# V's product in the recurrence as four 32x32 tiles on the diagonal instead of one 128x128 matmul

## The reference, cut to what matters

```
Wx = x @ W.T, normalised over all B*T rows, scaled by gamma, shifted by beta
Vt = V.T                                 # 32 x 32
def step(yt, wx_t):
    yt = sigmoid(wx_t + yt @ Vt)
    return (yt, yt)
_, ys = scan(step, zeros(B, H), Wx in order of t)
```

## Time and profile before

| | us |
|---|---|
| median of 3 runs | 905.27 (901.69 to 906.05) |
| the profiled execution, its own time | 901.04 |
| its span, first to last instruction | 899.3 |
| mean granted TensorE clock over the span | 0.956 of full speed |
| TensorE matmul busy (PE) | 708.9 (79%) |
| VectorE busy (DVE) | 721.3 (80%) |
| GpSimd busy (POOL) | 516.2 (57%) |
| ScalarE busy (ACT) | 369.3 (41%) |

### The profile page before, as it was taken

How to read it: one execution, slowest core, us unless ns; L and a number is a source line. 1 busy time by engine, 2 the same in 40 slices (tenths; PEclk the granted TensorE clock), 3 DMA queues, 4 the chain that set the end, 5 groups by cost and what they waited for, 6 DMA issues and landing times. The chain is left out here.

```text
span 899.3 us, 19137 instructions
## 1 busy us (share of the span) xinstructions
PE 708.9 (79%) x7722; PEld 442.3 (49%) x7722; DVE 721.3 (80%) x938; ACT 369.3 (41%) x585; POOL 516.2 (57%) x407
## 2 busy tenths in 40 slices
PE   7987886699877387788878878887887787787696
PEld 3554553356554154544544544454454454446363
DVE  3998887763320489999999989999999999974998
ACT  2220002156536755545555555555455554321000
POOL 5000000000010489999999999999999999970043
PEclk9999998889989799999999999999999999998799
DMA  4000000000004256666666665666667666600001
GB/s 162 5 4 4 5 4 2 3 1 1 1 1 126 74 171 210 197 187 190 212 194 188 197 203 177 189 209 196 189 189 213 187 198 205 195 30 1 0 12 41
DMA packets 55866, 102.81 MB, mean 114 GB/s; under 512 B 11169, under 2 KB 13345, under 8 KB 55777
## 3 DMA queue, kind: packets, MB, share of 16 engines
q1 hardware_dynamic: 55552, 100.73, 36.6%
q0 software_dynamic: 224, 0.85, 0.2%
HBM read 98.00 MB, written 3.54 MB: 113 GB/s over the span
## 5 line engine op out<-in xcount | busy, mean ns | idle before, releaser
L546 POOL TENSOR_TENSOR ring<-ring,big 128x576 f32<-128x576 f32 x206 | 285.1, 1406 | 13.7 <-DVE ring L936 11.8
L184 PE MATMUL banks<-ring,main_params 128*128 128x288 f32 x824 | 244.2, 426 | 4.6 <-POOL ring L546 2.8
L936 DVE TENSOR_TENSOR_SCAN ring<-big,banks 128x576 f32<-128x576 f32 x154 | 202.6, 1340 | 2.3
L184 PEld LDWEIGHTS banks<-ring,main_params 128*128 128x128 f32 x824 | 146.4, 192 | 60.0 <-POOL ring L546 15.7
L924 DVE TENSOR_TENSOR banks<-banks,big 128x576 f32<-128x576 f32 x192 | 143.0, 745 | 24.0 <-PE banks L1218 21.4
L718 ACT ACTIVATE big<-big,small 128x576 f32<-128x576 f32 x192 | 142.2, 764 | 27.3 <-DVE ring L936 21.5
L523 POOL COPY big<-normed 128x288 f32<-128x288 f32 x8 | 3.0, 429 | 244.2 <-DVE normed L422 244.2
L1217 PE MATMUL banks<-big,selectors 96*128 96x512 bf16 x192 | 74.5, 390 | 80.0 <-DVE ring L936 37.4
L356 PE MATMUL banks<-big 32*32 32x288 f32 x3712 | 96.9, 429 | 21.3 <-issue 17.2
L790 DVE SCALAR_TENSOR_TENSOR big<-big 128x288 f32<-128x288 f32 x216 | 93.6, 512 | 0.0
L718 ACT ACTIVATE banks<-big,small 128x576 f32<-128x576 f32 x64 | 47.4, 741 | 108.2 <-DVE ring L936 86.9
(11 more groups left out here) (166 smaller groups left out, 962.5 us busy)
## 6 DMA issues: line engine op xcount, KB each, us to landing
big<-bc_rows SPq DMA_DIRECT2D x640, 144.0 KB, 3.2
bc_rows<-big SPq DMA_DIRECT2D x16, 144.0 KB, 2.4
residual<-x_in SPq DMA_DIRECT2D x2, 576.0 KB, 5.8
out<-big SPq DMA_DIRECT2D x2, 512.0 KB, 3.0
main_params<-main_in SPq DMA_DIRECT2D x1, 895.0 KB, 8.7
big<-front_in POOLq DMA_DIRECT2D x1, 574.5 KB, 5.7
experts<-experts_in SPq DMA_DIRECT2D x1, 512.0 KB, 9.0
row_selectors<-rows_in POOLq DMA_DIRECT2D x1, 256.0 KB, 5.9
```

The source lines that it names most:

```text
L184: last = nc.tensor.matmul(PS[rows, 2 * p + a, 0:HALF], lhsT, rhs[:, bass.ds(at + a * HALF, HALF)], start=start, stop=stop, skip_group_chec ...
L546: nc.gpsimd.tensor_tensor(slot, slot, CT[n % 10], ALU.mult).then_inc(weighted, 1)
L936: nc.vector.tensor_tensor_scan(slot, DECAY[m % 3], place, 0.0, ALU.mult, ALU.add).then_inc(scanned, 1)
```

## The change

In each step of each set the one 128x128 matmul becomes four matmuls of 32x32, one for each group of channels. Each takes its group's block of `par("vt")`, its group's 32 rows of `YP` and writes the same 32 partitions of the same PSUM bank, for the same 88 to 96 columns. Only the last one raises `rec_mm[h]`. The keep-warm matmul stays as it is.

```diff
--- before.py
+++ after.py
@@ -1128,8 +1128,11 @@
                         pe.wait_ge(driven[h], q // GROUP + 1)
                     if q >= 1:
                         pe.wait_ge(rec_y[h], q)
-                    nc.tensor.matmul(step_place(k, h), par("vt"), at_step(YP, k, 0, images_of(h)), start=False, stop=True,
-                                     skip_group_check=True).then_inc(rec_mm[h], 1)
+                    for g in range(GROUPS):
+                        rows = slice(C * g, C * (g + 1))
+                        last = nc.tensor.matmul(step_place(k, h)[rows], par("vt")[rows, rows], at_step(YP, k, 0, images_of(h))[rows],
+                                                start=False, stop=True, skip_group_check=True)
+                    last.then_inc(rec_mm[h], 1)
                     keep_warm(1, 128)
             pe.wait_ge(ndiff_set, 1)
             nc.tensor.matmul(PS[0:1, 0, 0:1], NDIFF, par("ones"), start=True, stop=True).then_inc(count_mm, 1)
```

## The result

| | before | after |
|---|---|---|
| median, us | 905.12 (901.69 to 906.05, 4 runs) | 920.88 (918.72 to 922.43, 4 runs) |
| ratio to before | | 1.0179, 95% interval 1.0145 to 1.0213 |
| span of the profiled execution | 899.3 | 919.6 |
| mean granted clock | 0.956 | 0.915 |
| recurrence, first load to last sigmoid's start | 187.54 to 240.50 = 52.96 | 186.30 to 256.67 = 70.37 |

The change makes the kernel 15.8 us slower. The forecast was 927 with a range from 909 to 936.

What follows compares the result with a forecast made beforehand. The recurrence was taken as bound by a loop of latencies, 1.02 us a step, and after the change by PE's queue. Profiled 901.0 + 22.4 = 923.4, raised by 4.2 to a median of 927.6, stated as 927, range 909 to 936.

Steps and rivals of the forecast that it cites:

- Step 1: Recurrence product: four tiles run beside each other, 0.51 us at the upper clock, one set's chain 0.06 shorter per step.
- rival C: Recurrence product: the four tiles run one after another, +101 us, about 1006 as a median; chance 0.04.
- loop of latencies: One set's product, sigmoid and the gaps between them in a recurrence step: 0.94 us after the change, no longer the bound.
- rival B: Recurrence: no cost at the shape change, 3.1 us less, 902 as a median; chance 0.05.
- Step 2: PE's queue in the recurrence: loads wait at each shape change, half step 0.60, +9.9 us at the upper clock.
- Step 3: Instruction issue in the recurrence: 36 instructions a step cost nothing of their own.
- Step 4: Clock in the recurrence: falls to the lower level soon after 188.5, half step 0.72 to 0.73, +22.9 us in all.
- rival A: Recurrence: the shape changes cost but the clock holds, 911, or 915 us as a median; chance 0.23.
- the pair of strided passes at the lower clock: Both passes of the recurrence's tiled product: taken as 0.35 us, near the floor of 0.31.
- +22.4: Whole recurrence: the predicted slowdown in us, 22.9 less some 0.5 for first steps at the upper clock.
- the 4.2 us between the profiled execution and its median: Whole kernel: the new median should lie as far above its own profiled execution, taking 923.4 to 927.6.

Runs made afterwards that it cites:

- fifth experiment: Changed kernel with each keep-warm matmul of 128 columns replaced by two of 512 columns; one profiled execution, recurrence 101.05 us.
- third experiment: Changed kernel with each keep-warm matmul turned into 8 tiles of 32x32 with 256 columns; 904.55 us, ratio to before 1.0021.

## Why the prediction was right, step by step

**Step 1, the product.** Its time is confirmed: 0.51 predicted with 92 columns at the upper clock; 0.50 with 90 in the fifth experiment. Four tiles that write one bank run beside each other; rival C (one after another, 1006 us) is out, eight passes take 0.54. What was wrong is that one set's chain gets 0.06 shorter: I kept the wide product's 0.04 up to the sigmoid, and behind the tiles it is 0.07 in every trace, so only about half is left. The loop of latencies at the upper clock is 0.97 and not 0.94. The forecast didn't suffer, because TensorE's queue and not this loop was the bound, but rival B's 3.1 us were never there: the two runs with one shape won 1.1 and 2.0.

**Step 2, the shape changes.** Confirmed in each term. In its first 3 us, at the upper clock and with 88 columns, the changed kernel's half step is 0.58; the fifth experiment's loads come 0.007 later for every two columns, so with 92 it is 0.60, as worked out from the earlier trace rows. Rival B, no cost at the change, is out. At the lower clock the stage takes 70.37 with the alternation and 51.90 without, 18.5 us. The run without it has no keep-warm at all, so these 18.5 us hold keep-warm's own work too; the third experiment shows that at the upper clock such work costs nothing in the product's shape, and no run has it at the lower clock.

**Step 3, issue.** The third experiment agrees: 28 instructions more in a step, and the step is shorter.

**Step 4, the clock.** That it would fall soon after 188.5 and stay down was right (0.50 from 190.0 to 256.7), which is what separates the forecast from rival A. My reason for it was only argued from the earlier trace rows; the experiments agree with it (the clock stayed up with keep-warm in tiles and with long keep-warm, it fell without any, with one a step, and with the wide product and keep-warm in tiles, each time with TensorE busy for most or all of the stretch), but they don't show how the chip decides.

**The term that was mis-sized** is the pair of strided passes at the lower clock. I took 0.35 with 92 columns, between a floor of 0.31 and a ceiling of 0.60, from the first step of the recurrence, 0.57 in records against 0.54. Measured with 92 columns the product is 0.53; less the fixed 0.20 and 0.02 for three more tiles that is 0.31, the floor itself. With 92 columns the half step was 0.68 instead of 0.72 to 0.73, and 104 of them make nearly all of the difference between +22.4 and the measured +17.4. The row that misled me was of a wide product, whose two loads take 0.29 and 0.33 at the lower clock (0.19 each at the upper); it said nothing of the passes alone.

**The whole.** 927.6 less the 5.0 of the recurrence is 922.6; measured 920.88, and the 1.7 that are left lie outside the recurrence, within what executions of one kernel differ by. Adding the 4.2 us between the profiled execution and its median was right in size but not for the reason given: the changed kernel's median doesn't lie above its own profiled execution (920.88 against 921.39). The first trace of the kernel before had the short last quarter, the changed kernel's has the long one, and that there was one to find I couldn't know from a single trace; here the forecast had some luck. As a summary, of the recurrence's +17.4: tiles for the wide product with one shape throughout are worth -1.1 (no keep-warm, lower clock) to -2.0 (keep-warm in tiles, upper clock), and the alternation with its keep-warm adds 18.5 at the lower clock. At the upper one it would be about 62 us for the stage, 104 half steps of 0.60, 9 more than before; that number is worked out, since no run held the clock with the short keep-warm beyond the first 3 us.

## What to carry to other kernels

Before a matmul is cut into tiles, look at what shares TensorE's queue with it: a filler matmul of another shape between two products costs the rest of the product and the rest of the filler each time, and two such pairs in a step turned a loop bound by latency (1.02 us) into one bound by the queue (1.35). If the filler is there for the clock, give it the product's shape, or ask whether the clock is still needed: with the tiles this stage took 51.9 us at 1.2 GHz and 51.0 at 2.4, where with the wide product it took 60.7 and 53.0. And when a stage that has won a microsecond doesn't show it in the whole, compare stage by stage over two traces of the same kernel; here executions of one kernel differed by 5 us in a stage that nobody had touched.

## What the runs showed that I had not expected

A matmul pass over columns 12 elements apart costs about the same at both clock levels: the pair, worked out from the product's time less its fixed part, took 0.30 with 92 columns at the upper one and 0.31 at the lower, while contiguous passes of 288 columns follow each other by 0.24 at the upper and by 0.48 at the lower (L1164 at 254.53 and 255.01 us in the trace of the tiles with keep-warm behind). So for the strided pass it isn't the array's clock alone that sets the pace at the upper level; the runs don't say what else.

The sigmoid starts 0.07 behind the end of the last tile's record, but 0.04 behind the wide product's, in every trace and at both clock levels. That takes back half of what the shorter product wins. The ends of matmuls are modelled in the profile, so whether the tiles' records end too early or their last matmul releases the sigmoid later isn't shown.

In the kernel of tiles without keep-warm the two sets no longer run half a step apart: their sigmoids run back to back (0.66 together). That costs nothing that can be seen, since the step of 0.98 is the loop of one set, 0.60 + 0.33 + 0.05.
